# An RWKV block times a mixture of experts on one core: the order inside a round of the block is changed on three queues

## The chip, the cores and the metric

The kernel runs on one core of a Trainium2 chip. The metric is the time of one execution on the device in microseconds (us), the median of three runs. A core has five engines with a queue (a program) each, and each executes its queue strictly in order: TensorE (PE, with its weight loads PEld), VectorE (DVE), ScalarE (ACT), GpSimd (POOL) and SyncE (SP, which here only starts DMAs). They wait for each other by semaphores.

## What is computed

The input x is 16 sequences of 512 tokens with 256 channels. From xn = layernorm(x) two branches are computed, s (an RWKV block) and g (a mixture of experts, MoE), and the result is x + s * silu(g). Cut to what matters:

```python
x = _ln(x, ln0_w, ln0_b); h = _ln(x, ln1_w, ln1_b)
xk, xv, xr = (h * tm + shift(h) * (1 - tm) for tm in (tmk, tmv, tmr))
k, v, r = xk @ Wk.T, xv @ Wv.T, xr @ Wr.T
x = x + (sigmoid(r) * wkv(-exp(time_decay), time_first, k, v)) @ Wo.T
h2 = _ln(x, ln2_w, ln2_b)
xk2, xr2 = (h2 * cm + shift(h2) * (1 - cm) for cm in (cmk, cmr))
kf = square(relu(xk2 @ Wfk.T))
s = x + sigmoid(xr2 @ Wfr.T) * (kf @ Wfv.T)
# MoE: softmax router over 8 experts, each expert takes its 1024 best tokens,
# a token goes to one expert; out = weight * (gelu(xn @ W1[e]) @ W2[e])
```

`wkv` is a recurrence over the 512 tokens of a sequence, here computed as scans along the free dimension.

## The kernel before, in words

The program is written for each engine by hand: an engine's queue is the order in which its code stands, and nothing moves it later. The RWKV part is a pipeline of 16 **rounds**, b = 0 to 15, one sequence each. A round b does three things at once: the wkv part and first residual of sequence b, the start (norms, turn, mixes, k/v/r projections) of sequence b + 1 ("ahead"), and the channel mixing ("ffn") of sequence b - 1. Rounds are written by a function `round_` on each engine; most run in hardware loops (`Fori`). After them come 72 tiles of the MoE.

Names used below, for one round, by engine:

- **PE**: `hidden` (eight chunks h = 0 to 7, xk2 @ Wfk.T in a split precision, L845, L847, L852), each into one of three banks of `psM`; chunk h may start when ACT's Relu of chunk h - 3 has emptied its bank. `receptance` (L863, two halves, waiting for the Relus of chunks 5 and 6). `channel_out(b-1, j)`, j = 0 to 3 (kf @ Wfv.T, L875; j = 0 waits for all eight squares). `turn1` and `turn2` (transposes of the normed rows, L780). `project_out` (@ Wo.T, L827, waits for `att_done` of DVE). `project` 0, 1 and 2 (k, v and r, L815, two units of 128 channels each; the second unit of k waits for `x2_done`, DVE's first residual, which reads the same banks). `extra(b, 0..3)`: four small pieces of routing work that answer to four on DVE.
- **ACT**: `logs` (two Ln with a table load, L574, after DVE's `wkv_state`), `shares` (a table load and four Tanh, L580 and L583, after DVE's `wkv_gap`, before `wkv_mix`), `relu` (L596) and `square` (L600) of the eight chunks, `norm1` (L510, needs `cf1_ready` from POOL), `affine1`, `affine2` (L518), `norm0` (L501, for two sequences ahead), `norm2` (L510, needs `cf2_ready`), `sigmoid_fr` (L608), `take_kvr` (L557, L555: six units out of `psM`), `exponents` (L562), `exps` (L566, L568), `split_mix` (L589, what `hidden` of the next round starts from).
- **DVE**: `wkv_state` (two scans, L1323), `embed_scale` and `embed_shift` (L1424, L1429), `wkv_gap` (L1330), `moments1` (L1259, L1263), `gate_out` and `residual2` (L1408, L1415), `wkv_mix` (ends with L1370, `att_done`), `mix1` (L1277, L1282: differences, then mixes for k, v, r), `residual1` (L1399 and moments), `wkv_start` (L1309 to L1317), `mix2` (L1277, L1282, L1301), and `extra` 0 to 3.
- **POOL**: `rstd1` and `rstd2` (L407 to L412) make `cf1` and `cf2` from the moments.

The `extra` work differs by round. Rounds 0 to 3: router logits and token statistics (PE 1.7 us at each point in rounds 0 to 2). Rounds 4 to 10: a binary search (one count on DVE and one tiny matmul on PE at each point). Round 11 (`SELECT_ROUND`): the choice of experts, with a long DVE chain `choose` at point 2. Round 12: `place_tokens` on DVE at point 0, some 10 us. Rounds 12 to 15 are the **listing rounds**: DVE's `list_part` at point 0 gives POOL 16 rows of the list, and POOL issues 16 indirect DMAs (L400) in the round, eight of them **before** `rstd1` and eight between `rstd1` and `rstd2`:

```python
                if listing:
                    add_to_list(b, 0)
                if ahead:
                    rstd1(b + 1)
                if listing:
                    add_to_list(b, 1)
```

## Time and profile before

| what | value |
|---|---|
| time before, median of 3 runs | 1147.42 us (1146.86 to 1148.62) |
| the profiled execution, its own time | 1145.82 us |
| its span, first to last instruction | 1144.0 us |
| PE / DVE / ACT / POOL busy | 1056.0 (92%) / 878.3 (77%) / 627.6 (55%) / 353.9 us (31%) |
| a round of the kind 4 to 10 (round 8) | 47.53 us |
| rounds 11, 12, 13 with 14, 15 | 54.24, 59.73, 96.02, 38.66 us |
| mean granted TensorE clock | 0.980 |

A round is counted here from PE's first matmul of `hidden` to the next round's. PE is busy for nearly the whole span, so what it waits for inside the rounds is what an order of the queues can change. Starts of instructions are exact in such a profile; a matmul's end is modelled, so idle time of PE is best read from one start to the next.

### The profile page before, as it was taken

How to read it: one execution, taken by the hardware profiler on the slowest of the kernel's cores; microseconds unless marked ns; L12 is line 12 of the kernel's file. 1: busy time of each engine (PE TensorE's matmuls, PEld its weight loads, DVE VectorE, ACT ScalarE, POOL GpSimd, SP SyncE). 2: the span in 40 equal slices, each digit the busy share in tenths (PEclk: the TensorE clock that was granted, in tenths of full speed). 3: DMA queues.
4: the chain of work that ended last, by engine and by line, in shares of the span. 5: the costliest groups of instructions: out<-in, count | busy, mean ns of one | idle time of the engine just before them, and what ended most of it. 6: DMA issues, size and time to landing. Idle time of an engine off the chain costs nothing.

```text
span 1144.0 us, 19481 instructions
## 1 busy us (share of the span) xinstructions
PE 1056.0 (92%) x5152; PEld 835.4 (73%) x5153; DVE 878.3 (77%) x1988; ACT 627.6 (55%) x1085; POOL 353.9 (31%) x403
## 2 busy tenths in 40 slices
PE   5689999999999999999998698989899999999997
PEld 5358777677766777767775577667788888888886
DVE  5899797988989889898898868786426666666664
ACT  2647466685765857658574557647333333433332
POOL 3122313100001000010000537364406555555563
PEclk9889999999999999999999899999999999999999
DMA  9422230110101101011010101053503333323220
GB/s 305 159 89 93 92 110 0 38 47 10 55 0 55 55 0 55 0 55 55 1 56 1 56 1 56 1 184 107 204 19 107 91 95 97 102 90 97 88 75 15
DMA packets 60054, 80.44 MB, mean 70 GB/s; under 512 B 7774, under 2 KB 47327, under 8 KB 60002
## 3 DMA queue, kind: packets, MB, share of 16 engines
q1 hardware_dynamic: 48658, 54.69, 14.7%
q0 software_dynamic: 11360, 25.32, 7.3%
q8 instruction: 17, 0.28, 0.1%
q14 instruction: 19, 0.16, 0.0%
...
## 4 chain that ended last, share of the span: by engine, by line
PE 55%; DVE 14%; issue 14%; ACT 11%; POOL 4%; DMA 1%; DVEq 1%; ACTq 0%; SPq 0%; POOLq 0%
PE psM L946 11%; PE psM L815 11%; PE psKV L875 11%; PE psM L957 5%; PE psR L957 5%; ACT arena L596 3%; PE psM L827 3%; DVE arena L1282 2%; POOL sorted_list L400 2%; PE psT L780 2%; ACT arena L600 2%; PE psT L936 2%; PE psR L736 2%; ACT L580 1%; ACT L574 1%
## 5 line engine op out<-in xcount | busy, mean ns | idle before, releaser
L875 PE MATMUL psKV<-arena 128*128 128x256 f32 x1024 | 236.0, 384 | 3.4 <-ACT arena L600 1.7
L875 PEld LDWEIGHTS psKV<-arena 128*128 128x128 f32 x1024 | 193.8, 192 | 42.6 <-issue 14.8
L815 PE MATMUL psM<-arena 128*128 128x512 f32 x384 | 174.2, 600 | 1.0
L407 POOL TENSOR_SCALAR lnw<-mv 128x4 f32<-128x4 f32 x32 | 8.8, 275 | 484.5 <-DVE mv L1263 484.3
L946 PE MATMUL psM<-arena 128*128 128x128 f32 x1152 | 144.3, 279 | 0.1
L946 PEld LDWEIGHTS psM<-arena 128*128 128x128 f32 x1152 | 135.8, 193 | 4.2 <-issue 1.8
L690 ACT ACTIVATE arena<-arena,info_t 128x256 f32<-128x256 f32 x72 | 43.1, 600 | 161.9 <-DVE info_t L1441 153.6
L815 PEld LDWEIGHTS psM<-arena 128*128 128x128 f32 x384 | 70.7, 192 | 81.7 <-issue 80.1
L467 POOL DMA_INDIRECT out_dram<-arena,out_idx x72 | 88.5, 1229 | 95.8 <-DVE row_idx L1436 81.9
L1282 DVE SCALAR_TENSOR_TENSOR arena<-arena,vecs 128x512 f32<-128x512 f32 x160 | 108.7, 746 | 0.0
L845 PE MATMUL psM<-mix_hi,wfk_hi 128*128 128x512 f32 x256 | 103.6, 405 | 2.5 <-ACT mix_hi L589 1.3
L510 ACT ACTIVATE arena<-s_ring,cf 128x256 f32 (+1 forms) x128 | 66.3, 591 | 68.0 <-POOL cf L412 68.0
L400 POOL DMA_INDIRECT sorted_list<-info_cur,place_cur x64 | 71.1, 1111 | 97.5 <-DVE info_cur L1239 78.6
L557 ACT ACTIVATE arena<-psM 128x512 f32<-128x512 f32 x64 | 36.5, 588 | 115.6 <-PE psM L815 115.6
L847 PE MATMUL psM<-mix_hi,wfk_lo 128*128 128x512 f32 x256 | 99.9, 390 | 0.0
L596 ACT ACTIVATE arena<-psM 128x512 f32<-128x512 f32 x128 | 74.1, 590 | 38.2 <-PE psM L852 38.0
L863 PE MATMUL psM<-arena 128*128 128x256 f32 x256 | 64.5, 396 | 24.5 <-ACT arena L596 24.5
L518 ACT ACTIVATE arena<-psT,vecs 128x512 f32<-128x512 f32 x64 | 46.4, 774 | 68.6 <-PE psT L780 68.6
L1507 DVE COPY arena<-arena 128x1024 f32 x72 | 50.4, 700 | 43.7 <-issue 41.7
L1277 DVE TENSOR_TENSOR arena<-arena 128x512 f32<-128x512 f32 x64 | 42.6, 692 | 53.3 <-ACT arena L518 53.3
L852 PE MATMUL psM<-mix_lo,wfk_hi 128*128 128x512 f32 x256 | 79.2, 390 | 0.7 <-DVE mix_lo L1301 0.7
L600 ACT ACTIVATE arena<-arena 128x512 f32<-128x512 f32 x128 | 77.1, 626 | 0.0
...
## 6 DMA issues: line engine op xcount, KB each, us to landing
...
out_dram<-arena,out_idx POOLq DMA_INDIRECT x72, 2.8
```

Of the source, the lines that this page charges most:

```text
L400: pool.indirect_dma_start(sorted_list[:, :], bass.IndirectOffsetOnAxis(place_cur[:, j:j + 1], axis=0), info_cur[:, j, :], None).then_inc(S ...
L467: pool.indirect_dma_start(out[:, :], bass.IndirectOffsetOnAxis(out_idx[i][:, 0:1], axis=0), out_t[i], None, bounds_check=T - 1, oob_is_err ...
L596: act.activation(kf2[:, h], psM[:, h % 3, :], ACT.Relu).then_inc(S["relu_done"], 1)
L600: act.activation(kf2[:, h], kf2[:, h], ACT.Square).then_inc(S["sq_done"], 1)
L815: ins = pe.matmul(psM[:, u % 3, :], w[:, k, c * P:(c + 1) * P], mixA[:, m, k, :], start=(k == 0), stop=(k == CH - 1))
L845: pe.matmul(psM[:, h % 3, :], wfk_hi[:, k, n], mix_hi[:, k, :], start=(k == 0), stop=False)
L847: pe.matmul(psM[:, h % 3, :], wfk_lo[:, k, n], mix_hi[:, k, :], start=False, stop=False)
L852: ins = pe.matmul(psM[:, h % 3, :], wfk_hi[:, k, n], mix_lo[:, k, :], start=False, stop=(k == CH - 1))
L875: ins = pe.matmul(psKV[:, j // 2, (j % 2) * C:(j % 2 + 1) * C], kf2[:, h, j * P:(j + 1) * P], wfv[:, h, :], start=(h == 0), stop=(h == HC ...
L946: ins = pe.matmul(psM[:, i % 2, f * P:(f + 1) * P], w1_t[i % 2][:, k, f * P:(f + 1) * P], xnT[i % 2][:, k, :], start=(k == 0), stop=(k == ...
L957: ins = pe.matmul(y_ps[i % 2], hT_t[i % 2][:, f, :], w2_sb[:, ds(w + f * C, C)], start=(f == 0), stop=(f == FK - 1))
L1282: ins = v.scalar_tensor_tensor(dst[:, c], dmix[:, c], vecs[:, c, V[m]:V[m] + 1], hT[:, c, 0:SEQ], ALU.mult, ALU.add)
```

## The change

The same instructions are issued (only loops are regrouped); their order in a round changes on ACT, PE and DVE. POOL and SP are untouched.

- ACT: `logs` come first, ahead of every Relu; `shares` come after Relu 2 (before: after Relu 5); squares are put off, the last four to the end; `norm1` comes ahead of Relu 6 (before: after all squares); `affine1` ahead of `sigmoid_fr`; `norm0` from ahead of `take_kvr` 0 to behind `take_kvr` 3; `exps` is split, its first half ahead of `take_kvr` 4; the last `take_kvr` closes the round.
- PE: `turn1` ahead of `channel_out` 0; `channel_out` 1 from ahead of `project_out` to behind `project` 0, 1; `extra` 0 from the end of `hidden` to behind chunk 4; `extra` 2 behind `turn2`; `extra` 3 ahead of `channel_out` 3.
- DVE: `embed_shift` directly behind `embed_scale`; `gate_out` ahead of `moments1`; `fetch` to the end of `wkv`; the r mix out of `mix1` (now `mix1_r`) to behind `residual1` and `extra` 2.

```diff
@@ ACT, round_
-                if ffn:
-                    relus(b - 1, 0, 1)
-                    squares(b - 1, 0)
                 logs(b)
                 if ffn:
-                    for h in range(2, 6):
+                    for h in range(2):
                         relus(b - 1, h)
-                        squares(b - 1, h - 1)
+                        squares(b - 1, h)
+                    relus(b - 1, 2)
                 shares(b)
                 if ffn:
-                    relus(b - 1, 6, 7)
-                    squares(b - 1, 5, 6, 7)
+                    relus(b - 1, 3, 4)
+                    squares(b - 1, 2)
+                    relus(b - 1, 5)
+                if ahead:
+                    norm1(b + 1)
+                if ffn:
+                    relus(b - 1, 6)
+                    squares(b - 1, 3)
+                    relus(b - 1, 7)
+                    squares(b - 1, 4, 5, 6, 7)
...
                 if ahead:
-                    norm1(b + 1)
+                    affine1(b + 1)
                 if ffn:
                     sigmoid_fr(b - 1)
                 if ahead:
-                    affine1(b + 1)
-                    if further:
-                        norm0(b + 2)
                     take_kvr(b + 1, 0, 2)
                 norm2(b)
                 if ahead:
                     take_kvr(b + 1, 2, 4)
+                    if further:
+                        norm0(b + 2)
                 affine2(b)
-                for c in range(CH):
-                    if ahead:
-                        take_kvr(b + 1, 4 + c, 5 + c)
-                        exponents(b + 1, c)
-                    split_mix(b, c)
                 if ahead:
-                    exps(b + 1)
+                    exp_past(b + 1)
+                    take_kvr(b + 1, 4, 5)
+                    exponents(b + 1)
+                split_mix(b, 0)
+                split_mix(b, 1)
+                if ahead:
+                    exp_now(b + 1)
+                    take_kvr(b + 1, 5, 6)
@@ PE, hidden and round_
-                extra(rnd, 0)
+                    if h == 4:
+                        extra(rnd, 0)
...
                     receptance(b - 1)
-                    channel_out(b - 1, 0)
...
                 if ahead:
                     turn1(b + 1)
-                if ffn and ahead:
-                    channel_out(b - 1, 1)
+                if ffn:
+                    channel_out(b - 1, 0)
                 project_out(b)
-                if not ahead:
-                    channel_out(b - 1, 1)
                 extra(b, 1)
                 if ahead:
                     project(b + 1, 0, 1)
+                if ffn:
+                    channel_out(b - 1, 1)
+                turn2(b)
                 extra(b, 2)
-                if ffn:
-                    channel_out(b - 1, 2)
-                turn2(b)
                 if ahead:
                     project(b + 1, 2)
                 if ffn:
+                    channel_out(b - 1, 2)
+                extra(b, 3)
+                if ffn:
                     channel_out(b - 1, 3)
-                extra(b, 3)
@@ DVE, wkv and round_
                 if ahead:
                     embed_scale(b + 1)
+                    embed_shift(b + 1)
                 extra(b, 0)
                 wkv_gap(b)
-                if ahead:
-                    embed_shift(b + 1)
-                    moments1(b + 1)
-                    if further:
-                        fetch(b + 2)
                 if not (isinstance(b, int) and b < 2):
                     gate_out(b - 2)
+                if ahead:
+                    moments1(b + 1)
...
                 extra(b, 2)
                 if ahead:
+                    mix1_r(b + 1)
                     wkv_start(b + 1)
```

The first place that the prediction speaks of is ACT's queue around the shares and norm1, in round 3 (every round has this order; L580 and L583 are the shares, L596 Relus, L600 squares, L510 the norm, L634 a softmax step that only round 3 has). Before:

```order
L596 ACTIVATE arena<-psM 128x512 [waits kf_done]
L600 ACTIVATE arena<-arena 128x512 [waits relu_done]
L580 ACT_TABLE_LOAD
L580 ACTIVATE arena<-arena,half_w 128x512 [waits gap_done] x2
L583 ACTIVATE arena<-arena,half_u 128x512 x2
L596 ACTIVATE arena<-psM 128x512 [waits kf_done] x2
L600 ACTIVATE arena<-arena 128x512 [waits relu_done] x3
L634 ACTIVATE desk<-desk 128x512 [waits route_exp_in]
L510 ACTIVATE arena<-s_ring,cf 128x256 [waits cf1_ready,tr2_done]
L510 ACTIVATE arena<-s_ring,cf 128x256 x3
```

The same place of the change, from Relu 2 on, where the Relu is L601, the square L605, and the shares are L585 and L588:

```order
L601 ACTIVATE arena<-psM 128x512 [waits kf_done]
L585 ACT_TABLE_LOAD
L585 ACTIVATE arena<-arena,half_w 128x512 [waits gap_done] x2
L588 ACTIVATE arena<-arena,half_u 128x512 x2
L601 ACTIVATE arena<-psM 128x512 [waits kf_done] x2
L605 ACTIVATE arena<-arena 128x512 [waits relu_done]
L601 ACTIVATE arena<-psM 128x512 [waits kf_done]
L510 ACTIVATE arena<-s_ring,cf 128x256 [waits cf1_ready,tr2_done]
L510 ACTIVATE arena<-s_ring,cf 128x256 x3
L601 ACTIVATE arena<-psM 128x512 [waits kf_done]
L605 ACTIVATE arena<-arena 128x512 [waits relu_done]
L601 ACTIVATE arena<-psM 128x512 [waits kf_done]
```

The shares moved ahead of Relus 3, 4 and 5, and the norm, with its wait for `cf1_ready`, ahead of Relus 6 and 7 and of five squares.

The second place is PE's queue behind `hidden` in the same round. Before, from the second half of `receptance` (L863) to the first unit of `project` (L815):

```order
L863 MATMUL psM<-arena 128x256 [waits relu_done]
L863 MATMUL psM<-arena 128x256 x3
L875 MATMUL psKV<-arena 128x256 [waits s_mult,sq_done]
L875 MATMUL psKV<-arena 128x256 x7
L780 MATMUL psT<-cst,arena 128x128 [waits hn1_ready,h2_ready]
L780 MATMUL psT<-cst,arena 128x128 x7
L875 MATMUL psKV<-arena 128x256 x8
L827 MATMUL psM<-arena 128x256 [waits sigf_done,relu_done,att_done]
L827 MATMUL psM<-arena 128x256 x7
L754 MATMUL psR<-cst,desk 128x128 [waits route_step]
L754 MATMUL psR<-cst,desk 128x128 x3
L815 MATMUL psM<-arena 128x512 [waits sigf_done,kvr_ready,mix1_done]
```

The same stretch of the change (L876 receptance, L792 the turn, L888 channel output, L839 output product, L766 an extra, L827 the projection):

```order
L876 MATMUL psM<-arena 128x256 [waits relu_done]
L876 MATMUL psM<-arena 128x256 x3
L792 MATMUL psT<-cst,arena 128x128 [waits hn1_ready,h2_ready]
L792 MATMUL psT<-cst,arena 128x128 x7
L888 MATMUL psKV<-arena 128x256 [waits s_mult,sq_done]
L888 MATMUL psKV<-arena 128x256 x7
L839 MATMUL psM<-arena 128x256 [waits sigf_done,relu_done,att_done]
L839 MATMUL psM<-arena 128x256 x7
L766 MATMUL psR<-cst,desk 128x128 [waits route_step]
L766 MATMUL psR<-cst,desk 128x128 x3
L827 MATMUL psM<-arena 128x512 [waits sigf_done,kvr_ready,mix1_done]
```

The turn now stands ahead of the channel output, and the second channel output is gone from this stretch: it stands behind the k and v projections.

## Rows read from the trace of the kernel before

**Rows 1.** Windows: stretch, us, busy PE, PEld, DVE, ACT, POOL; PEclk, DMA, GB/s
```profile
427.43:474.96 47.53, 45.65 (x195) 34.02 (x194) 41.53 (x86) 31.89 (x55) 4.57 (x8) 1.00 0.10 33
570.03:624.27 54.24, 48.70 (x200) 35.42 (x198) 48.89 (x86) 32.22 (x55) 3.56 (x8) 0.97 0.09 30
624.27:684.00 59.73, 49.46 (x186) 36.88 (x185) 46.27 (x88) 31.35 (x55) 24.59 (x24) 0.89 0.10 27
684.00:780.02 96.02, 89.33 (x370) 66.27 (x369) 74.25 (x127) 62.16 (x105) 48.45 (x48) 1.00 0.23 72
780.02:818.68 38.66, 34.16 (x154) 27.65 (x153) 22.54 (x47) 20.89 (x35) 26.28 (x32) 1.00 0.58 193
```

**Rows 2.** Timeline of PE, round 8: start, us, instruction, idle and releaser
```profile
433.89 0.61 PE L852 MATMUL psM<-mix_lo,wfk_hi 128*128 128x512 f32 x2
434.58 0.50 PE L845 MATMUL psM<-mix_hi,wfk_hi 128*128 128x512 f32 x1
...
438.98 1.97 PE L863 MATMUL psM<-arena 128*128 128x256 f32 x8
442.47 1.99 PE L863 MATMUL psM<-arena 128*128 128x256 f32 x8 [1.52 <-ACT arena L596]
444.60 3.69 PE L875 MATMUL psKV<-arena 128*128 128x256 f32 x16
...
456.05 7.50 PE L815 MATMUL psM<-arena 128*128 128x512 f32 x16
...
467.94 3.60 PE L815 MATMUL psM<-arena 128*128 128x512 f32 x8
```

**Rows 3.** Timeline of ACT, round 8: the shares, Relus 6 and 7, last squares
```profile
438.08 1.28 ACT L580 ACT_TABLE_LOAD   x1
...
441.84 1.06 ACT L596 ACTIVATE arena<-psM 128x512 f32<-128x512 f32 x2
442.80 1.66 ACT L600 ACTIVATE arena<-arena 128x512 f32<-128x512 f32 x3
```

**Rows 4.** Timeline of DVE, round 8: wkv_state and the end of wkv_mix
```profile
427.81 2.34 DVE L1323 TENSOR_TENSOR_SCAN arena<-arena 128x512 f32<-128x512 f32 x2 [1.10 <-ACT arena L568]
...
448.75 1.28 DVE L1370 SCALAR_TENSOR_TENSOR arena<-arena 128x512 f32<-128x512 f32 x2
```

**Rows 5.** Timeline of PE, rounds 11 and 12: extra 2, then receptance's second half
```profile
610.03 2.07 PE L768 MATMUL psR<-desk,cst 128*128 128x512 f32 x2 [4.09 <-DVE desk L1170]
...
643.16 3.78 PE L863 MATMUL psM<-arena 128*128 128x256 f32 x8 [5.28 <-ACT arena L596]
```

**Rows 6.** Timeline of DVE, round 13: list_part gives POOL its rows
```profile
688.17 0.18 DVE L1239 COPY info_cur<-info 128x64 int32<-128x64 int32 x1
```

**Rows 7.** Timeline of POOL, round 13: first list DMA, rstd1; a DMA of round 15
```profile
689.16 1.09 POOL L400 DMA_INDIRECT sorted_list<-info_cur,place_cur  x1 [15.52 <-DVE info_cur L1239]
...
701.17 0.27 POOL L407 TENSOR_SCALAR lnw<-mv 128x4 f32<-128x4 f32 x1
...
784.84 0.96 POOL L400 DMA_INDIRECT sorted_list<-info_cur,place_cur  x1 [0.30 <-issue]
```

**Rows 8.** Timeline of ACT: norm1 in rounds 12 and 13
```profile
653.40 2.07 ACT L510 ACTIVATE arena<-s_ring,cf 128x256 f32 x4 [8.26 <-POOL cf L412]
...
704.24 2.08 ACT L510 ACTIVATE arena<-s_ring,cf 128x256 f32 x4 [3.12 <-POOL cf L412]
```

**Rows 9.** Timeline of DVE, round 1: wkv_state
```profile
87.58 2.34 DVE L1323 TENSOR_TENSOR_SCAN arena<-arena 128x512 f32<-128x512 f32 x2 [0.98 <-ACT arena L568]
```

**Rows 10.** Timeline of POOL: rstd2 begins, in rounds 8 and 13
```profile
460.29 0.20 POOL L407 TENSOR_SCALAR lnw<-mv 128x4 f32<-128x4 f32 x1 [19.12 <-DVE mv L1263]
...
717.74 0.90 POOL L407 TENSOR_SCALAR lnw<-mv 128x4 f32<-128x4 f32 x1 [2.51 <-DVE mv L1263]
```

**Rows 11.** Timeline of ACT: norm2 in round 13
```profile
722.07 2.07 ACT L510 ACTIVATE arena<-s_ring,cf 128x256 f32 x4 [3.58 <-POOL cf L412]
```

**Rows 12.** Timeline of PE, round 15: turn2
```profile
813.30 1.09 PE L780 MATMUL psT<-cst,arena 128*128 128x128 f32 x8 [0.32 <-ACT arena L510]
```

More of the change, by code:

```diff
@@ L557, in take_kvr, with exponents, exp_past, exp_now @@
                         act.activation(dst, src, ACT.Copy).then_inc(S["kvr_ready"], 1)
-            def exponents(b, c):
-                wait_run(act, S["pre_done"], b * CH + (c + 1))
-                act.activation(E2[:, c], qb[c], ACT.Relu, bias=wneg[:, c:c + 1]).then_inc(S["relu2_done"], 1)
-            def exps(b):
+            def exponents(b):
+                for c in range(CH):
+                    wait_run(act, S["pre_done"], b * CH + (c + 1))
+                    act.activation(E2[:, c], qb[c], ACT.Relu, bias=wneg[:, c:c + 1]).then_inc(S["relu2_done"], 1)
+            def exp_past(b):
+                wait_run(act, S["pre_done"], b * CH + CH)
                 act.activation(E1, E1, ACT.Exp).then_inc(S["exp_done"], 1)
+            def exp_now(b):
                 wait_run(act, S["relu2_done"], b * CH + CH)
@@ L663, in _ @@
             take_kvr(0, 2, 4)
-            exponents(0, 0)
-            exponents(0, 1)
-            exps(0)
+            exp_past(0)
+            exponents(0)
+            exp_now(0)
             take_kvr(0, 4, 6)
@@ L1270, in moments1, with change @@
                 st.end()
-            def mix(b, ready, step, outs):
-                st = Steps(v, S[step], CH, b, S["waited"])
+            def change(b, ready, st):
                 for c in range(CH):
@@ L1277, in mix @@
                     st.then(v.tensor_tensor(dmix[:, c], hT[:, c, 1:SEQ + 1], hT[:, c, 0:SEQ], ALU.subtract))
-                for i, (dst, m, done) in enumerate(outs):
-                    for c in range(CH):
-                        if i == 0:
-                            st.wait(c + 1)
-                        ins = v.scalar_tensor_tensor(dst[:, c], dmix[:, c], vecs[:, c, V[m]:V[m] + 1],
-                                                     hT[:, c, 0:SEQ], ALU.mult, ALU.add)
-                        if done == "mixk_done":
-                            ins.then_inc(S[done], 1)
-                    if done != "mixk_done":
-                        ins.then_inc(S[done], 1)
-                st.end()
+            def mix(c, dst, m):
+                return v.scalar_tensor_tensor(dst[:, c], dmix[:, c], vecs[:, c, V[m]:V[m] + 1],
+                                              hT[:, c, 0:SEQ], ALU.mult, ALU.add)
             def mix1(b):
@@ L1392, in wkv @@
                     extra(b, 1)
+                if ahead and further:
+                    fetch(b + 2)
             def residual1(b):
@@ L1477, in _ @@
             mix1(0)
+            mix1_r(0)
             v.wait_ge(S["pow_ready"], 16)
```

27 lines of the change are left out of this document (24 added, 3 removed).

## Prediction, made blind

> **What bounds the kernel now.** I read the windows first, one stretch per round, to see where PE is not busy. PE is busy 45.7 of the 47.5 us of a round like round 8, but only 48.7 of 54.2 in round 11, 49.5 of 59.7 in round 12 and 89.3 of 96.0 in rounds 13 and 14 together [rows 1]. DVE is busy 41.5 us of round 8, so PE is the bound there and its waits are the time to be had. The timeline of PE, start to start, then gives these waits in round 8 [rows 2]: chunk 5 of hidden comes 0.69 us after two matmuls whose pace is 0.23 each (0.24 lost, Relu 2); receptance's second half 3.49 us after the first, whose own work is 2.13 less 0.40, or 1.73 (1.76 lost, Relu 6); the first channel_out 0.40 late (squares); and the four k and v units take 7.50 us where twice the two r units (3.60 each) would be 7.2 (0.3 lost, x2_done). That is 2.7 us, with some 0.2 more in the slower first matmuls behind each wait (0.50 in the second row for a usual 0.39): 2.9 of 47.5 us, so 44.6 us of PE work.
>
> The timelines of ACT and DVE say why. A table load and four Tanh hold ACT from 438.08 to 441.84, 3.76 us, while Relus 6 and 7 are due; the squares end at 444.46 [rows 3]. DVE's state scan starts 0.4 us after PE's round (427.81 against 427.43), and att_done is at 450.03, 22.6 us into the round [rows 4], which PE asks for only at 25.0.
>
> In the listing rounds POOL sets the pace: round 13 starts at 684.00, list_part ends at 688.35 [rows 6], the eight DMAs take from 689.16 to 701.17, 12.0 us [rows 7], rstd1 3.1 us more, and norm1 starts at 704.24, 20.2 us into the round [rows 8]. Before, ACT had all Relus and squares behind it by then, and PE lost 1.5 us at turn1 alone.
>
> **The change, part by part** (times from PE's start of the round, R; durations as in round 8).
>
> *Shares earlier, rounds 3 to 10.* Relu 2 starts 4.4 after R and ends at 5.0. Then the shares, 3.76, so Relu 3 ends at 9.35. Chunk 6, due at 8.4, waits 1.0 (with a slow start 1.15). Relus 4, 5 and square 2 take ACT to 10.7, norm1 (2.0) to 12.7, Relus 6, 7 and the squares at 0.5 each to 16.4. PE, 1.0 late, ends hidden at 12.25, receptance at 15.7, turn1 at 16.6: neither receptance nor channel_out 0 waits. The second residual of rows that PE's k projection needs is no longer late, since the r mix (1.3 us) is behind it. What hides the late squares is turn1 (0.9 us), with 0.2 to spare; without it each us late is a us.
>
> This needs the gap by 5.0 and cf1 by 10.7. DVE's state must start early. At the end of a round ACT now has the first Exp, take_kvr 4 and both exponents ahead of the mixes' split and the second Exp; turn2 ends some 10.8 us before the round does, and affine2 (1.45), 1.04, 0.55, 1.3, 1.1 and 1.0 us bring exp_now's end to 3.7 us before R, since channel_out 2 and 3 (6.9 us) now both stand behind turn2. From -3.7, DVE's 2.3 (state), 2.6 (embedding with its own wait), 1.75 (extra 0) and 0.6 end the first gap at 3.5; gate_out and moments1 end at 7.2, POOL's 3.1 make cf1 ready at 10.3. Wkv_mix (8.9 us, to 450.03 in [rows 4]) then ends at 17.2 against PE's need at 20.1: moving channel_out 1 away from project_out costs nothing while that holds. A round is 44.6 + 1.15 = 45.7, against 47.53: -1.8. I take -1.85 for the eight rounds 3 to 10: **-14.8**.
>
> *Round 11.* PE waited 4.09 us for choose and restarted at half clock, 2.07 us for two matmuls that take 1.0 in that form at the round's end [rows 5]. Extra 2 now stands behind channel_out 1 and turn2, 4.3 us later, and choose ends just then. With the common gain: 48.35 against 54.24: **-5.9**. DVE leaves the round late, though, only 1.3 us ahead of R.
>
> *Rounds 12 to 14: the price.* ACT's queue is in order, and norm1 now stands ahead of Relus 6 and 7 and five squares. Queued behind its wait for cf1 are those; PE's receptance waits for Relu 6, and everything of PE behind it. In round 13 DVE starts at -3.5: state and embedding end at 1.4, list_part at 1.7, the first DMA 0.8 later, 12.0 for eight, 3.1 for rstd1: norm1 starts at 17.5, 2.7 earlier than before, ends at 19.5, Relu 6 at 20.0. PE was due there at 14.0 and stands for 6 us. After 5.28 idle us the same eight matmuls took 3.78 instead of 1.99 us [rows 2, 5] at a granted clock of half (0.89 over round 12, [rows 1]); I take 2.1 for the restart, between 1.7 and 2.8 (half of one or of the two half-speed stretches there). From Relu 6: 1.83 + 2.1 + 0.87 (turn1) + 3.46 + 3.46 (channel_out 0, project_out) + 21.7 for the rest = 33.4, so 53.4 a round where it was 48.0 (96.02 / 2): **+10.9** for two. Round 12: place_tokens (10.2 us) starts 4.0 after R, the list is there at 14, norm1 at 29.3 (15.3 later, as before from 638.07 to 653.40 [rows 8]), the rest as in round 13: 65.2 against 59.73: **+5.4**.
>
> *Rounds 1, 2, 15.* In round 1 the state starts late (87.58, 1.5 after R, [rows 9]; 1.0 in the change), now ahead of all Relus. The logs end at 4.7, so chunk 3 waits 0.9; the gap comes at 8.5, Relu 3 ends at 12.9, chunk 6 waits 1.9. Less the small stalls that go: +2.2. Round 2 has 1.7 us of router work behind chunk 4, which covers the shares: -1.0. In round 15 channel_out 2 no longer covers the way from project_out to turn2 (7.5 us, turn2 at 813.30 [rows 12]): 4 us idle and a slow restart, against att waited for no more and mix_lo no longer late: +0.3. Together **+1.5**. The embeddings', fetch's and sigmoid's moves fall into slack of DVE and ACT. The tail after round 15 is unchanged and starts as late as the round ends.
>
> Sum: -14.8 - 5.9 + 10.9 + 5.4 + 1.5 = -2.9. Of the profiled execution (span 1144.0, 1145.82 with what lies around it) that makes 1142.9; the median is 1.6 higher, 1147.42, so **1144.5**.
>
> **The rivals.** (A) The forecast.
>
> (B) The state does not run ahead as worked out: DVE's and ACT's end of round slips by 1.2 us or more, because small waits between three queues (0.2 each time an engine waits for its own or another's semaphore, [rows 1 to 3] show some) add up along affine2, mix2, split and Exp. For it: I have slack of only 0.2 to 0.4 us at the squares and at cf1. Then nine rounds pay 0.4 each at the squares and three listing rounds 1.2 each, since there the state is on the path: +7, **1152**, slower. It decides for slower from about 0.8 us of slip.
>
> (C) rstd2 in rounds 12 and 13. It took longer under DVE's scans: the first row 0.90 against 0.20 us, norm2 at 722.07, 4.3 after it began [rows 10, 11], against 2.9. I took 3.3, as the r mix now lies beside its first half. If it stays 4.3, norm0, now ahead of affine2, pushes that back by 1.35, and rounds 13 and 14 each pay it through the list: +2.7, **1147.2**, no change. The Trainium skill, SBUF — State Buffer, section "SBUF: two separate sides", says that a GpSimd operation is fully blocked while a DVE instruction with two SBUF inputs holds the port they share; the r mix is such an instruction, so by that rule the whole of rstd2 is slowed and C is the case. The 0.90 against 0.20 us agrees, but 0.27 in round 13's rstd1 beside another such instruction [rows 7] doesn't, which is why C stays a rival.
>
> (D) The listing rounds cost less: the DMAs come every 1.26 us (0.96 and 0.30, as in round 15, where DVE has little to do, [rows 7]), not 1.5, and one restart is missed: -6, **1138.5**. Against it: DVE works beside them as before.
>
> That the change does nothing is excluded: the queues differ in every round.
>
> **How the numbers follow.** A 0.50 (own range 1141 to 1149: restarts 1.7 or 2.8 four times, 0.2 a round in eight), B 0.22, C 0.18, D 0.10. The likeliest gives 1144.5. The range 1138 to 1153 takes in D, C and most of B. A measurement here can tell about 0.2%, 2.3 us. A lies past that bound by 0.6 only: 0.30 of its 0.50 counts as faster, 0.16 as same, 0.04 as slower. With D faster is 0.40, and I add 0.04 for part of C and B's lower end gone; same 0.29, slower 0.27.
>
> **What would show it.** Rounds 4 to 10 at 45.7 us with one wait of PE, 1.0 us at chunk 6, none at receptance; DVE's state scan 3.7 us ahead of PE's round; no wait at extra 2 in round 11; PE idle 6 us at receptance in rounds 13 and 14 with norm1 released by POOL and half clock behind it; round 12 at 65 us. Wrong would be: project_out waiting for att_done, channel_out 0 waiting for squares by more than 0.5 us, or a state scan less than 2.5 us ahead.

## The result and the profile after

The change makes the kernel slower: 1152.3 us (median, 1150.93 to 1153.96), a ratio of 1.0043 to the kernel before (95% interval 1.003 to 1.0056). The profiled execution took 1152.11 us with a span of 1150.3, which is 6.3 more than before. The windows of the profile after, stretch by stretch as in [rows 1] (us; busy PE, PEld, DVE, ACT, POOL; PEclk; DMA share; GB/s), say where. As in the prediction, R is PE's start of a round.

```profile
425.38:472.28 46.90, 45.41 (x195) 34.22 (x193) 41.23 (x87) 32.14 (x55) 5.48 (x8) 1.00 0.11 34
566.08:615.01 48.93, 47.17 (x199) 34.92 (x197) 46.63 (x86) 30.22 (x53) 5.18 (x8) 1.00 0.11 32
615.01:679.02 64.01, 48.69 (x186) 36.30 (x185) 46.99 (x90) 32.48 (x55) 24.40 (x24) 0.87 0.09 26
679.02:787.05 108.03, 93.47 (x370) 69.97 (x369) 74.83 (x132) 63.87 (x107) 48.91 (x49) 0.94 0.21 64
787.05:826.28 39.23, 34.49 (x154) 29.19 (x153) 20.67 (x43) 18.54 (x31) 27.57 (x32) 0.96 0.65 212
```

Round 8 is 0.6 us shorter than before, round 11 5.3; round 12 is 4.3 longer, rounds 13 and 14 together 12.0, round 15 0.6. One more pair of windows gives rounds 3 to 10 together, of the kernel before and then of the change:

```profile
189.69:570.03 380.34, 365.15 (x1539) 272.21 (x1538) 334.03 (x687) 255.42 (x433) 36.07 (x64) 1.00 0.10 32
```
```profile
192.40:566.08 373.68, 362.71 (x1539) 273.79 (x1537) 330.49 (x682) 257.21 (x433) 43.40 (x64) 1.00 0.11 33
```

That is -6.7 where -14.8 was forecast, and POOL, which the diff does not touch, is busy 7.3 us longer over the same 64 instructions. The timeline of PE in round 8 (R = 425.38), beside [rows 2]:

```profile
434.86 0.50 PE L857 MATMUL psM<-mix_hi,wfk_hi 128*128 128x512 f32 x1 [0.70 <-ACT arena L601]
...
437.72 1.89 PE L876 MATMUL psM<-arena 128*128 128x256 f32 x8
440.10 1.99 PE L876 MATMUL psM<-arena 128*128 128x256 f32 x8 [0.49 <-ACT arena L601]
441.93 1.04 PE L792 MATMUL psT<-cst,arena 128*128 128x128 f32 x8
443.28 1.10 PE L888 MATMUL psKV<-arena 128*128 128x256 f32 x4 [0.30 <-ACT arena L605]
```

Chunk 6 waits for Relu 3 behind the shares (0.87 from start to start beyond its pace), as forecast. Receptance's second half waits for Relu 6 (0.65) and channel_out 0 for the squares (0.48, as turn1 alone takes 0.87); neither was forecast. The timeline of ACT at that place, beside [rows 3]:

```profile
430.47 1.28 ACT L585 ACT_TABLE_LOAD   x1
...
435.71 0.59 ACT L601 ACTIVATE arena<-psM 128x512 f32<-128x512 f32 x1
437.50 2.08 ACT L510 ACTIVATE arena<-s_ring,cf 128x256 f32 x4 [1.19 <-POOL cf L412]
439.48 0.57 ACT L601 ACTIVATE arena<-psM 128x512 f32<-128x512 f32 x1
```

Norm1 stands 1.19 us for cf1, with Relus 6 and 7 and five squares behind it. It starts at R + 12.1; the forecast had 10.7. The timelines of POOL and DVE:

```profile
433.05 1.17 POOL L407 TENSOR_SCALAR lnw<-mv 128x4 f32<-128x4 f32 x1 [23.60 <-DVE mv L1275]
434.29 0.27 POOL L408 TENSOR_SCALAR lnw<-mv 128x4 f32<-128x4 f32 x1
434.74 1.57 POOL L410 TENSOR_TENSOR cf<-lnw,minus_half 128x4 f32<-128x4 f32 x1 [0.18 <-POOL lnw L408]
436.49 0.69 POOL L412 TENSOR_TENSOR cf<-lnw,cf 128x4 f32<-128x4 f32 x1 [0.18 <-POOL cf L410]
```
```profile
432.48 0.38 DVE L1275 BATCH_NORM_AGGREGATE mv<-bnst 128x2 f32<-128x6 f32 x4
432.95 1.22 DVE L1442 TENSOR_TENSOR s_ring<-s_ring,arena 128x1024 f32 x1
434.09 0.76 DVE L1367 TENSOR_SCALAR arena<-arena 128x512 f32<-128x512 f32 x2
434.76 1.28 DVE L1370 SCALAR_TENSOR_TENSOR arena<-arena 128x512 f32<-128x512 f32 x2
```

A POOL operation on 4 elements per partition takes 1.17 us, and ends as DVE's residual2 (L1442) ends (434.22 against 434.17). The pow (L410) takes 1.57 instead of 1.01 beside the next DVE products of two SBUF tiles. All of rstd1 takes 4.13 us. In the kernel before it took 2.80 in the same round: its first operation lay beside gate_out (L1408), and only its last one, L412, met residual2 (L1415). That one took 0.98 us and ended with it too (441.17 against 441.12). POOL, then DVE, before:

```profile
438.37 0.19 POOL L407 TENSOR_SCALAR lnw<-mv 128x4 f32<-128x4 f32 x1 [23.01 <-DVE mv L1263]
...
440.19 0.98 POOL L412 TENSOR_TENSOR cf<-lnw,cf 128x4 f32<-128x4 f32 x1 [0.18 <-POOL cf L410]
```
```profile
439.89 1.23 DVE L1415 TENSOR_TENSOR s_ring<-s_ring,arena 128x1024 f32 x1 [0.32 <-DVE arena L1408]
```

In the listing rounds norm1 starts 28.5 us after R in round 12 and 18.3 in round 13 (ACT's timeline, beside [rows 8]):

```profile
643.55 2.07 ACT L510 ACTIVATE arena<-s_ring,cf 128x256 f32 x4 [8.52 <-POOL cf L412]
...
697.35 2.07 ACT L510 ACTIVATE arena<-s_ring,cf 128x256 f32 x4 [7.39 <-POOL cf L412]
```

and PE stands at receptance for it, and then runs slowly (timeline of PE, beside [rows 5], and the window from that point):

```profile
646.16 3.63 PE L876 MATMUL psM<-arena 128*128 128x256 f32 x8 [5.19 <-ACT arena L601]
...
699.96 3.78 PE L876 MATMUL psM<-arena 128*128 128x256 f32 x8 [6.67 <-ACT arena L601]
703.53 1.33 PE L792 MATMUL psT<-cst,arena 128*128 128x128 f32 x8
```
```profile
699.90:705.90 6.00, 5.94 (x22) 5.00 (x23) 0.03 (x1) 3.99 (x9) 4.48 (x6) 0.65 0.03 2
```

A granted clock of 0.65 over 6.0 us is 2.1 us of work lost, the figure of the forecast (in round 12 it was 0.72 over 6.0 us, 1.7 lost). Two more places are rstd2 in round 13 (POOL, beside [rows 10]) and the state scan of round 13, 2.26 us ahead of R = 679.02 (DVE):

```profile
715.08 0.49 POOL L407 TENSOR_SCALAR lnw<-mv 128x4 f32<-128x4 f32 x1 [7.08 <-DVE mv L1275]
715.64 1.66 POOL L408 TENSOR_SCALAR lnw<-mv 128x4 f32<-128x4 f32 x1
717.49 1.78 POOL L410 TENSOR_TENSOR cf<-lnw,minus_half 128x4 f32<-128x4 f32 x1 [0.18 <-POOL lnw L408]
```
```profile
676.76 2.34 DVE L1349 TENSOR_TENSOR_SCAN arena<-arena 128x512 f32<-128x512 f32 x2
```

### The profile page after: what moved, and what is told of

Same layout as the page of the kernel before. It is cut to its first block, busy times and chain, and to the rows that moved or that the text cites. A ratio compares the mean times of both kernels' runs of the same rounds, so it can differ in the third digit from the quotient of the medians.

```text
span 1150.3 us, 19481 instructions
## 1 busy us (share of the span) xinstructions
PE 1054.7 (92%) x5152; PEld 840.3 (73%) x5153; DVE 874.5 (76%) x1988; ACT 630.1 (55%) x1085; POOL 373.3 (32%) x403
## 4 chain that ended last, share of the span: by engine, by line
PE 54%; DVE 19%; issue 11%; ACT 7%; POOL 6%; DMA 1%; DVEq 1%; ACTq 0%; SPq 0%; POOLq 0%
PE psM L958 11%; PE psKV L888 10%; PE psM L827 8%; PE psM L969 5%; PE psM L839 5%; PE psR L969 5%; DVE arena L1349 3%; PE psM L876 2%; POOL sorted_list L400 2%; ACT arena L510 2%; DVE arena L1292 2%; POOL cf L410 2%; DVE bnst L1271 2%; PE psT L948 2%; PE psT L792 2%
## 5 line engine op out<-in xcount | busy, mean ns | idle before, releaser
L888 PE MATMUL psKV<-arena 128*128 128x256 f32 x1024 | 232.5, 381 | 4.1 <-ACT arena L605 4.1
L888 PEld LDWEIGHTS psKV<-arena 128*128 128x128 f32 x1024 | 193.1, 191 | 43.8 <-issue 17.5
L827 PE MATMUL psM<-arena 128*128 128x512 f32 x384 | 174.0, 603 | 0.0
L407 POOL TENSOR_SCALAR lnw<-mv 128x4 f32<-128x4 f32 x32 | 17.0, 531 | 466.5 <-DVE mv L1275 466.3
L958 PEld LDWEIGHTS psM<-arena 128*128 128x128 f32 x1152 | 134.3, 192 | 4.4 <-issue 1.9
L827 PEld LDWEIGHTS psM<-arena 128*128 128x128 f32 x384 | 71.8, 193 | 79.1 <-issue 77.8
L857 PE MATMUL psM<-mix_hi,wfk_hi 128*128 128x512 f32 x256 | 106.4, 416 | 21.6 <-ACT arena L601 21.4
L510 ACT ACTIVATE arena<-s_ring,cf 128x256 f32 (+1 forms) x128 | 66.3, 589 | 79.5 <-POOL cf L412 79.5
L601 ACT ACTIVATE arena<-psM 128x512 f32<-128x512 f32 x128 | 73.7, 587 | 34.8 <-PE psM L864 32.4
L876 PE MATMUL psM<-arena 128*128 128x256 f32 x256 | 66.3, 408 | 21.8 <-ACT arena L601 21.7
L876 PEld LDWEIGHTS psM<-arena 128*128 128x128 f32 x256 | 51.2, 204 | 34.1 <-ACT arena L601 26.2
L857 PEld LDWEIGHTS psM<-mix_hi,wfk_hi 128*128 128x128 f32 x256 | 48.6, 190 | 37.4 <-ACT arena L601 27.8
```

The costliest lines, as they stand in the source:

```text
L510: ins = act.activation(hn[:, j], xs[:, j * C:(j + 1) * C], ACT.Identity, scale=cf[:, 0, j:j + 1], bias=cf[:, 1, j:j + 1])
L827: ins = pe.matmul(psM[:, u % 3, :], w[:, k, c * P:(c + 1) * P], mixA[:, m, k, :], start=(k == 0), stop=(k == CH - 1))
L857: pe.matmul(psM[:, h % 3, :], wfk_hi[:, k, n], mix_hi[:, k, :], start=(k == 0), stop=False)
L876: ins = pe.matmul(psM[:, (HC + u) % 3, (j % 2) * C:(j % 2 + 1) * C], mixB_r[:, k, j * P:(j + 1) * P], wfr[:, k, :], start=(k == 0), stop=( ...
L888: ins = pe.matmul(psKV[:, j // 2, (j % 2) * C:(j % 2 + 1) * C], kf2[:, h, j * P:(j + 1) * P], wfv[:, h, :], start=(h == 0), stop=(h == HC ...
L958: ins = pe.matmul(psM[:, i % 2, f * P:(f + 1) * P], w1_t[i % 2][:, k, f * P:(f + 1) * P], xnT[i % 2][:, k, :], start=(k == 0), stop=(k == ...
```

## The experiments

The two theories. **1:** norm1 now stands early in ACT's in-order queue, so that what delays cf1 delays PE; in rounds 3 to 10 it is rstd1 beside residual2 (a DVE swap that looked free), in the listing rounds the eight DMAs ahead of rstd1. **2:** other places of the new order cost the time. The experiments ran in three groups, each on a chip of its own beside the kernel before, which takes 1155.1 us on the chip of e1 to e4, 1157.2 on that of e5 to e8 and 1156.0 on that of e9 to e12 (medians). The change's rounds in e5 differ from those above by at most 0.2 us, but for round 15; what follows round 15 takes 3 to 10 us longer in the experiments' profiles (327 to 334 us) than above (324.0). So ratios and round lengths are compared. Lengths in us, each from one profiled execution (the first two rows from the profiles above), ratio to the kernel before with its 95% interval. The diffs below are cut to the steps that move; conditions and loop headings are left out.

| kernel | rounds 5 to 10 | 11 | 12 | 13, 14 | 15 | ratio |
|---|---|---|---|---|---|---|
| before | 47.53 | 54.2 | 59.7 | 48.2, 47.9 | 38.7 | 1 |
| the change | 46.90 | 48.9 | 64.0 | 54.2, 53.8 | 39.2 | 1.0043 (1.003 to 1.0056) |
| e1_moments_first | 45.63 | 47.3 | 64.1 | 54.0, 54.0 | 39.2 | 0.9974 (0.9964 to 0.9984) |
| e2_listing_old | 46.90 | 48.9 | 58.8 | 51.6, 51.3 | 39.5 | 0.9955 (0.9942 to 0.9968) |
| e3_listing_norm_late | 46.90 | 48.9 | 62.2 | 51.1, 50.7 | 39.5 | 0.9969 (0.9956 to 0.9981) |
| e4_norm0_back | 46.90 | 48.9 | 65.9 | 52.4, 53.2 | 39.4 | 1.0017 (1.0007 to 1.0026) |
| e5_change_again | 46.90 | 48.9 | 63.8 | 54.1, 53.8 | 41.1 | 1.0027 (1.0015 to 1.0039) |
| e6_before_swap | 47.17 | 60.4 | 59.6 | 48.7, 47.3 | 40.1 | 1.0002 (0.9984 to 1.002) |
| e7_residual_first | 47.19 | 57.9 | 65.8 | 59.3, 60.1 | 39.3 | 1.0203 (1.0182 to 1.0223) |
| e8_best | 45.63 | 47.3 | 61.1 | 47.7, 47.4 | 40.4 | 0.9796 (0.9782 to 0.9811) |
| e9_sigmoid_first | 45.63 | 47.3 | 58.8 | 46.6, 46.4 | 39.2 | 0.9764 (0.9748 to 0.978) |
| e10_list_round | 45.65 | 47.3 | 55.4 | 46.4, 46.4 | 35.5 | 0.9741 (0.9727 to 0.9754) |
| e11_shares_late | 48.0 to 49.1 | 49.9 | 65.2 | 54.2, 54.1 | 39.3 | 1.0207 (1.0191 to 1.0224) |
| e12_norm_late | 47.19 | 48.6 | 62.5 | 51.2, 51.3 | 39.4 | 1.0037 (1.0024 to 1.0051) |

**e1_moments_first.** The change with one pair of DVE steps back:

```diff
+                if ahead:
+                    moments1(b + 1)
                 gate_out(b - 2)
-                if ahead:
-                    moments1(b + 1)
                 residual2(b - 2)
```

> The change, but on DVE moments1 stands ahead of gate_out and residual2 again. Theory 1 (POOL is slowed by the DVE instruction beside it): in the change, rstd1 of rounds 4 to 10 runs beside residual2's add of two SBUF tiles and takes 4.1 us from its first to its last operation instead of 2.8; with moments1 first it runs beside gate_out, which reads PSUM, and takes 2.8 to 3.0. Rounds 4 to 10 fall from 46.9 to 45.8 to 46.0 us, the whole to about 1144.5 us, with no wait of PE at receptance. Theory 2 (the order of ACT and PE itself is too tight, POOL's speed is nothing): rstd1 still takes 4 us or PE still waits 0.6 us at receptance; rounds fall by at most 0.3 us, the whole stays above 1150 us.

Rounds 5 to 10 fall by 1.27 us to 45.63, the forecast's 45.7, and the ratio is 0.9974 (1144.5 us, as expected, would be 0.997 of 1147.7). POOL's and DVE's timelines of round 8 (R = 420.89) show why: residual2 is the same, but rstd1 now begins beside gate_out, which reads one of its inputs from PSUM.

```profile
427.44 0.19 POOL L407 TENSOR_SCALAR lnw<-mv 128x4 f32<-128x4 f32 x1 [22.47 <-DVE mv L1275]
427.69 0.19 POOL L408 TENSOR_SCALAR lnw<-mv 128x4 f32<-128x4 f32 x1
428.07 1.01 POOL L410 TENSOR_TENSOR cf<-lnw,minus_half 128x4 f32<-128x4 f32 x1 [0.18 <-POOL lnw L408]
429.25 0.75 POOL L412 TENSOR_TENSOR cf<-lnw,cf 128x4 f32<-128x4 f32 x1 [0.18 <-POOL cf L410]
```
```profile
427.18 1.22 DVE L1434 SCALAR_TENSOR_TENSOR arena<-arena,psKV 128x1024 f32<-128x1024 f32 x1
428.71 1.23 DVE L1441 TENSOR_TENSOR s_ring<-s_ring,arena 128x1024 f32 x1 [0.32 <-DVE arena L1434]
```

Rstd1 takes 2.56 us instead of 4.13, and no wait is left but chunk 6's.

The edit moves two things, though: the moments also end 1.1 us earlier (6.4 after R instead of 7.5), so that cf1 comes 2.7 earlier (9.1 instead of 11.8). How far each of the two counts, other rounds tell. In rounds 4 to 10 of the change and of e7 the round is as long as cf1's end, counted from R, plus 35.1: 11.34 and 46.45, 11.63 and 46.73, 11.80 and 46.90, 12.08 and 47.19. With cf1 at 10.5 or earlier it would be at its floor of 45.6 (an estimate from these four and from e1). Round 3 of the change has the slow rstd1 (3.63 us) behind early moments (5.6), cf1 at 9.5, and loses nothing: 45.83, as in e1. And a rstd1 of 2.56 us behind the change's own moments would end at 10.2. So it takes both, the later moments, which the forecast had (7.2), and the slow rstd1, which it hadn't. No run has the late moments with a fast rstd1.

**e6_before_swap.** The kernel before, with the change's DVE swap alone:

```diff
+                    gate_out(b - 2)
                 moments1(b + 1)
-                    gate_out(b - 2)
                     residual2(b - 2)
```

> The kernel before with one thing of the change: on DVE gate_out stands ahead of moments1 and residual2 behind it, so that POOL's rstd1 lies beside residual2. Theory 1 (rstd1 is slowed beside residual2, and this costs time only since norm1 now stands early on ACT): cf1 is ready some 2.5 us later, but norm1 still waits behind the squares that end 3 us after cf1; rounds 4 to 10 stay at 47.5 us, listing rounds as before, ratio 1.000 (0.998 to 1.002). Theory 2 (the swap itself costs DVE or PE time, wherever norm1 stands): rounds 4 to 10 at 48.5 or more, ratio 1.006 or more.

Rounds 4 to 10 don't suffer, since norm1 stands behind the squares there; they are even 0.36 us shorter, by the k and v units (6.95 us from start to start instead of 7.34). Cf1 comes 1.4 us later, not 2.5: rstd1 takes 3.30 us in round 8, since its first operation starts 0.14 us ahead of residual2 (438.34 against 438.48) and takes 0.19, and the second, started at 438.60, takes 1.16 and ends with residual2 (439.76 against 439.71). But round 11 grows by 6.2, which neither theory had: norm1 waits 6.6 us for cf1 and PE 5.1 us at turn1. The profile is of an execution 2.3 us above the median of the 12 runs, which lie between 1152.2 and 1164.9 us, so how often round 11 is that long isn't known. POOL's timeline of round 11, then DVE's:

```profile
580.21 3.98 POOL L407 TENSOR_SCALAR lnw<-mv 128x4 f32<-128x4 f32 x1 [24.37 <-DVE mv L1263]
584.25 1.05 POOL L408 TENSOR_SCALAR lnw<-mv 128x4 f32<-128x4 f32 x1
585.49 5.49 POOL L410 TENSOR_TENSOR cf<-lnw,minus_half 128x4 f32<-128x4 f32 x1 [0.18 <-POOL lnw L408]
```
```profile
579.98 1.22 DVE L1417 TENSOR_TENSOR s_ring<-s_ring,arena 128x1024 f32<-128x1024 f32 x1
...
588.83 1.29 DVE L1370 SCALAR_TENSOR_TENSOR arena<-arena 128x512 f32<-128x512 f32 x2
590.03 0.15 DVE L1133 TENSOR_SCALAR desk<-psR 128x1 f32<-128x1 f32 x1
```

Beside DVE's unbroken run of large products and scans one small POOL operation takes 5.49 us, not 1.01.

**e7_residual_first.** The change with `residual2` ahead of `moments1`, so that rstd1 meets wkv_mix:

```diff
                     gate_out(b - 2)
+                    residual2(b - 2)
                 moments1(b + 1)
-                    residual2(b - 2)
```

> The change with moments1 behind residual2 (order on DVE: gate_out, residual2, moments1, wkv_mix), so that rstd1 lies beside wkv_mix: one product with a single input, then products and scans of two SBUF inputs. Theory 1 (every DVE instruction with two SBUF inputs holds POOL up): rstd1 is as slow as in the change, 4 us, and 1.2 us later: rounds 4 to 10 at 47.5 to 48.1 us (46.9 in the change), ratio to before 1.010 to 1.014. Theory 2 (residual2 alone, a single instruction of 1024 elements, held it up): rstd1 takes 2 us, cf1 comes 1.2 us earlier than in the change: rounds at 46.0, ratio 0.998.

In rounds 4 to 10 neither number comes out: rstd1 takes 2.87 us, between the theories, it starts 1.5 us later than in the change, and a round takes 47.19. The ratio, 1.0203, is worse than either said, through rounds 11, 13 and 14. In round 11 rstd1 takes 9.95 us. In rounds 13 and 14 it is the DMAs ahead of it that stretch (POOL's timeline of round 14): the fifth takes 5.67 us while wkv_mix runs on DVE, the sixth, behind it, 0.96:

```profile
763.52 5.67 POOL L400 DMA_INDIRECT sorted_list<-info_cur,place_cur  x1 [0.30 <-issue]
769.50 0.96 POOL L400 DMA_INDIRECT sorted_list<-info_cur,place_cur  x1 [0.30 <-issue]
```

So it is not residual2 alone that holds POOL up, and not rstd1 alone that is held up. The Trainium skill, SBUF — State Buffer, section "SBUF: two separate sides", has the rule: a DVE instruction with two SBUF inputs locks the port pair that it shares with GpSimd for its whole length, against a GpSimd operation that reads SBUF. The 1.17 beside residual2, the 0.19 beside gate_out and, in e6, the 0.19 of the operation that started ahead of residual2 and the 1.16 of the next one agree. That POOL stays out over several such instructions in a row (5.49 us here) goes beyond it, and isn't constant: beside the same DVE sequence L407 took 0.25 us in round 8 of this kernel and 2.78 in its round 11. What decides that stays open.

**e2_listing_old, e3_listing_norm_late.** Two ways to take the listing rounds back. In e2 ACT and PE run rounds 12 to 15 in the order before, DVE in the new one. In e3 only norm1 goes back, in rounds 12 to 14:

```diff
                 if ffn:
                     relus(b - 1, 5)
-                if ahead:
-                    norm1(b + 1)
                 if ffn:
                     relus(b - 1, 6)
                     squares(b - 1, 3)
                     relus(b - 1, 7)
                     squares(b - 1, 4, 5, 6, 7)
+                if ahead:
+                    norm1(b + 1)
```

> The change, but ACT and PE run rounds 12 to 15 in the order of before (DVE keeps the new order). Theory 1 (in the listing rounds norm1's wait for POOL now blocks Relu 6 and all of PE behind it): rounds 13 and 14 fall from 54 to 46.4 us each, below the 48 of the kernel before, because the list reaches POOL earlier; round 12 from 64.0 to about 59.6, round 15 to about 38.7. The whole: about 1132 us. Theory 2 (the listing rounds are long because POOL's DMAs or the clock are slower with DVE's new order): rounds 12 to 14 stay at or above the 59.7, 48.2 and 47.9 of before, the whole 1140 us or more.

> The change, but in rounds 12 to 14 norm1 stands behind all squares on ACT again; PE keeps turn1 ahead of channel_out 0. Theory 1: receptance no longer waits, turn1 waits instead until norm1 is done (about 20.4 us into round 13) and everything behind it too; only receptance's half with its restart is won, about 2 us a round: rounds 13 and 14 at 52, the whole about 1146.5 us. So the larger part of the loss is turn1's place on PE. Theory 2 (norm1's place on ACT is the whole loss): rounds 13 and 14 at 47 to 48 us, the whole about 1134 us.

Norm1's place alone is worth 3.1 us in each of rounds 13 and 14 (51.1 and 50.7, nearer to theory 1's 52 than to theory 2's 47 to 48), e2 2.5. E2 falls short of its 46.4 because of a thing that I had not reckoned: DVE's new order has embed_shift ahead of list_part, and ACT's old end of a round makes the state late again (0.72 us after R), so that the list comes later than in the kernel before. PE loses 3.3 us at turn1 in round 13 of e2. Both are still some 3 us or more a round behind the kernel before.

**e4_norm0_back.** ACT's norm0 as before, ahead of `take_kvr` 0, so that it doesn't push affine2 (rival C):

```diff
+                    norm0(b + 2)
                     take_kvr(b + 1, 0, 2)
                 norm2(b)
                 if ahead:
                     take_kvr(b + 1, 2, 4)
-                    norm0(b + 2)
```

> The change, but norm0 stands ahead of take_kvr 0 again. Theory 1 (rstd2 slowed by the r mix and the scans makes norm2 late, and norm0 behind it pushes affine2 and so DVE's state scan back): DVE's scan is 3.5 us ahead of rounds 13 and 14 instead of 2.26, and rounds 13 and 14 are 1.2 us shorter each; rounds 4 to 10 unchanged; the whole about 1149.8 us. Theory 2 (norm0's place is hidden): rounds 13 and 14 stay at 54.2 and 53.8, the whole at 1152.3 us.

The scan of rounds 13 and 14 comes 1.5 us earlier (3.76 ahead of R), as C has it, and the rounds fall by 1.8 and 0.6, together the 2.4 of theory 1. Round 12 of this profile is 1.9 longer, but ahead of the place where norm0 moved: the eighth DMA took 1.50 us instead of 0.96, and behind the wait at receptance the granted clock was 0.50 over 6.0 us, 3.0 lost, instead of 0.72. The ratio, 1.0017, is below the change's 1.0043, but its interval overlaps that of e5 (1.0027), so what the move is worth in the sum isn't shown.

**e5_change_again.** The change itself on the chip of the second group.

> The change itself once more, beside the kernel before on the chip of these experiments, so that what the single edits are worth can be set against it. Both theories expect the ratio measured first, 1.004 (1.003 to 1.0056), and the same rounds: 4 to 10 at 46.9 us, 12 at 64.0, 13 and 14 at 54.

The intervals of the two ratios overlap; the rounds are the same but for round 15 (41.1 against 39.2).

**e8_best, e9_sigmoid_first, e10_list_round.** What the runs pointed to, built up. E8 is e1 with norm1 late in rounds 12 to 14 as in e3, and two more edits for the listing rounds, on PE and DVE:

```diff
@@ PE, rounds 12 to 14
+                channel_out(b - 1, 0)
                 turn1(b + 1)
-                channel_out(b - 1, 0)
                 project_out(b)
@@ DVE, rounds 13 to 15
                 wkv_state(b)
+                extra(b, 0)
                 embed_scale(b + 1)
                 embed_shift(b + 1)
-                extra(b, 0)
```

> Built from what the first four runs showed: the change with moments1 ahead of gate_out, and in the listing rounds norm1 behind the squares on ACT (12 to 14), turn1 behind channel_out 0 on PE (12 to 14), and list_part ahead of the two embedding steps on DVE (13 to 15). Theory 1 (each loss is a place in a queue, and the places are independent): rounds 4 to 10 at 45.6; in round 13 the scan starts 3.5 us ahead, list_part ends 0.9 ahead, eight DMAs to 12, rstd1 to 15, norm1 to 17 and PE asks for the turn at 19.5, so rounds 13 and 14 at 45.5 to 47; round 12, where place_tokens still delays the list, 58 to 60; ratio to before 0.976 to 0.980. Theory 2 (POOL's sixteen DMAs and two rstd bound a listing round whatever the order): rounds 13 and 14 at 50 or more, ratio 0.985 or more.

Theory 1 holds in the main: the ratio is 0.9796 as expected, rounds 13 and 14 are at 47.7 and 47.4 (expected 45.5 to 47), round 12 is at 61.1 (58 to 60). Which of the new edits brings how much of the 3.2 to 3.4 us against e3 no run separates. PE's project_out still waits there, though att_done is long there (timelines of PE and ACT in round 13):

```profile
688.89 1.32 PE L843 MATMUL psM<-arena 128*128 128x256 f32 x5 [2.20 <-issue]
```
```profile
686.82 1.45 ACT L518 ACTIVATE arena<-psT,vecs 128x512 f32<-128x512 f32 x2 [1.71 <-issue]
688.15 1.08 ACT L613 ACTIVATE arena<-psM 128x512 f32<-128x512 f32 x2
```

It starts as ACT's sigmoid_fr (L613) reads the banks out, which the change put behind affine1. E9 puts it ahead of norm1 in those rounds:

```diff
+                    sigmoid_fr(b - 1)
                     norm1(b + 1)
                 affine1(b + 1)
-                sigmoid_fr(b - 1)
```

> The version of the run before (e8_best) with one more edit: in rounds 12 to 14 ACT's sigmoid_fr stands ahead of norm1, where ACT is idle 1.4 us for cf1. There PE's project_out came 2.26 us late in rounds 13 and 14, with att_done 6 us old. Theory 1 (it waits for sigmoid_fr, which the change put behind affine1 and so behind the turn): that wait goes, rounds 13 and 14 at 45.4 us (47.65 and 47.44 in e8_best), round 12 some 2 shorter; ratio to e8_best 0.995. Theory 2 (it waits for something else): rounds as in e8_best.

That wait goes, and half of the gain is given back one step on: PE reaches the k projection 0.9 us before mix1 is ready. Rounds 13 and 14 fall by 1.1, not 2.2, and round 12 by 2.3.

E10 adds four edits, in round 12 on POOL above all:

```diff
@@ POOL, round 12
+                    rstd1(b + 1)
                     add_to_list(b, 0)
-                    rstd1(b + 1)
+                    rstd2(b)
                     add_to_list(b, 1)
-                rstd2(b)
```

> e9_sigmoid_first with the four remaining losses edited in one kernel: in rounds 1 and 12 ACT's old order up to the squares (shares behind Relu 5), in round 12 rstd1 on POOL ahead of the list's DMAs and rstd2 between its two halves, in round 15 channel_out 2 ahead of turn2 on PE. Theory 1 (in round 12 the eight DMAs between the list and rstd1 are what is waited for, so that rstd1 ahead of them frees norm1 some 10 us earlier, and place_tokens alone, 10 us on DVE, remains): round 12 at 52 to 55 us (61.15 in e8_best), round 1 at 52.3 (54.1), round 15 at 38 to 38.7 (40.4); ratio to before 0.965 to 0.970. Theory 2 (the sixteen DMAs that now all come behind rstd1 run into round 13 and hold its list up): round 13 longer by what round 12 gains, ratio 0.975.

The windows of rounds 12, 13 with 14, and 15 (e10):

```profile
609.47:664.85 55.38, 49.07 (x186) 36.40 (x185) 47.27 (x90) 33.47 (x56) 24.79 (x24) 0.91 0.11 30
664.85:757.59 92.74, 89.22 (x370) 66.29 (x369) 74.81 (x132) 63.45 (x106) 49.95 (x49) 1.00 0.25 74
757.59:793.07 35.48, 33.38 (x154) 27.89 (x152) 18.86 (x41) 18.53 (x31) 26.55 (x32) 1.00 0.64 211
```

Round 12 is at 55.4 (expected 52 to 55), 3.5 less than in e9, and round 13 is no longer, so theory 2 falls; how much of the 3.5 is POOL's new order and how much ACT's old one there no run separates. Round 15 gains 3.7 by channel_out 2 ahead of turn2 (with the change's order it took between 39.2 and 41.1 in the profiles). The ratio, 0.9741, misses the 0.965 to 0.970, by round 1 above all: with the old ACT order and PE's turn1 early it takes 58.6 instead of 54.1, as PE waits 1.1 at receptance and 3.1 for the turn. Left alone there, by that difference, the kernel would be some 4 us faster still; that was not run. As it stands, 1126.6 us against 1156.0 is the fastest of all.

**e11_shares_late, e12_norm_late.** Each takes one of ACT's two early moves out of e1 in all rounds:

```diff
@@ e11
-                shares(b)
                 relus(b - 1, 3, 4)
                 squares(b - 1, 2)
                 relus(b - 1, 5)
+                shares(b)
                 norm1(b + 1)
@@ e12
-                norm1(b + 1)
                 relus(b - 1, 6)
                 ...
                 squares(b - 1, 4, 5, 6, 7)
+                norm1(b + 1)
```

> The change with moments1 ahead of gate_out (as e1_moments_first, rounds 4 to 10 at 45.6 us), and the shares back behind Relu 5. It prices the shares' new place. Theory 1: chunk 6 no longer waits (0.9), but the shares end at 12.3 us in the round and Relu 6, behind norm1, at 14.8, when PE asks for it at 13.0: receptance waits 1.8, rounds at 46.5 to 46.9. Theory 2 (the shares' place is indifferent): 45.6.

> The change with moments1 ahead of gate_out (as e1_moments_first), and norm1 behind the squares on ACT in all rounds, PE's order as in the change (turn1 ahead of channel_out 0). It prices norm1's new place in rounds 4 to 10, the same move that costs 6 us in a listing round. Theory 1: Relu 7 ends at 12.6, the squares at 14.9, norm1 at 16.9, and PE asks for the turn at 15.7: a wait of 1.2 there, rounds at 46.6 to 46.9 (45.6 with norm1 early); rounds 13 and 14 at 51 or less. Theory 2 (norm1 early brings nothing in these rounds): 45.6.

E11 costs 2.4 to 3.5 us a round, more than the 0.9 to 1.3 expected: Relu 5 itself has to wait for chunk 5, so that receptance waits 2.7, not 1.8, and in rounds 8 and 9 half clock behind that wait (last section) adds 1.1. E12 costs 1.56 (expected 1.0 to 1.3), a wait of 1.5 at turn1. So both moves earn their place in rounds 4 to 10, and e12 has the listing rounds at 51.2, where e1 has 54.0: the same move is worth +1.6 in one kind of round and -2.8 in another.

## Why the prediction was wrong

The forecast was a gain of 2.9 us; the change costs 4.6 by the medians (1147.7 before in the same runs), 6.3 by the profiles. By the terms, forecast and then measured (before to after): rounds 3 to 10 -14.8 and -6.7; round 11 -5.9 and -5.3; round 12 +5.4 and +4.3; rounds 13 and 14 +10.9 and +12.0; rounds 1, 2 and 15 +1.5 and +1.9 (+2.3, -1.0, +0.6). Two places had no term: what stands ahead of round 1, +1.4, and the tail, -1.3 (forecast unchanged). The sum of the measured is +6.3. Two of the forecast's differences are a tenth off by its own numbers (2 x 53.4 - 96.02 is 10.8, 65.2 - 59.73 is 5.5); they cancel.

**The step that failed** is in the rounds 3 to 10: "gate_out and moments1 end at 7.2, POOL's 3.1 make cf1 ready at 10.3", with "durations as in round 8". The moments ended at 7.5, but rstd1's duration is not its own: the 3.1 was read where the neighbour of its first operation, gate_out, had an input in PSUM, and the change puts residual2 with two SBUF inputs there. From the moments' end to cf1 it was 4.3 us instead of 3.1, cf1 came at 11.8 instead of 10.3 and norm1 at 12.1 instead of 10.7. The row of L412 in the kernel before (0.98 us, over with residual2) showed the effect already. I had the slack (0.2 to 0.4) right, and with it used up the delay came through to PE: 46.90 instead of 45.7, and 45.63 in e1, whose rstd1 has gate_out beside it and whose moments end earlier. With 45.63 in rounds 4 to 10 and 47.3 in round 11 the sum would have been about -4, a small gain, and e1 measures just that, 0.9974. I applied the port rule to rstd2 in rival C and didn't ask it of rstd1, whose neighbour the diff itself swaps. Round 3 came out right (45.83), although rstd1 took 3.63 us there: the moments ended 1.9 earlier, which hid it.

**The rivals.** B, the state scan slipping, was not it: it ran 3.44 ahead of R where 3.7 was forecast, and 1.44 ahead of round 12, where 1.3 was. B's price, the squares' and cf1's small slack, was paid for another reason. C is right in its mechanism: rstd2 took 4.7 and 4.6 us in rounds 12 and 13, the scan came only 2.26 us ahead of rounds 13 and 14 (3.5 forecast), and e4 undoes that. It priced itself at 2.7 over the forecast for rounds 13 and 14; they came 1.1 over it. D did not come. The mechanism of A in the listing rounds is shown by e3, e8 and e12: norm1 and all behind it wait for POOL, PE stood 6.7 us at receptance in round 13 (6 forecast), restarted at half clock and lost 2.1 (2.1 forecast).

**Smaller.** Round 12: norm1 came 28.5 after R, not 29.3, and in round 13 18.3, not 17.5. Ahead of round 1: it starts at 87.46 (86.04 before), but with the same order up to there it started at 86.2 in the profiles of e4 and e5 and at 87.2 to 88.4 in those of e1 to e3 and e7 to e12, and at 86.6 with the old order in e6. The start varies by 2 us, and how much of this +1.4 is the change's stays open. Round 11: the wait at extra 2 is gone, as forecast. Round 15: turn2 waits 3.77, 4 forecast. "The embeddings', fetch's and sigmoid's moves fall into slack" was wrong for two of them, hidden by the larger wait: embed_shift delays the list (e2), and sigmoid_fr stands in project_out's way as soon as receptance no longer waits (e8, e9).
